# Identity matmuls into an unread PSUM bank, between TensorE's steps in the two closing stages of a two-layer transformer tower

## What is computed

```python
out = attn.reshape(b, n, f) @ W_out + b_out      # 192 x 192
h = h + out
x = _layernorm(h, axis=-1)                       # input of the experts
route = jax.nn.softmax(x @ router_w + router_b)  # 8 experts
```

## Time and profile before

| | |
|---|---|
| median of 3 runs | 1840.75 us (1835.26 to 1847.22) |
| the profiled execution's own time | 1849.49 us |
| its span, first to last instruction | 1847.8 us |
| mean granted clock of TensorE over the span | 0.899 |
| TensorE busy in the span | 1621.7 us (88%) |
| VectorE, ScalarE, GpSimd busy | 1098.9, 613.7, 429.0 us |
| closing stage 0, first to last record | 748.76 to 829.36 us |
| closing stage 1, first to last record | 1315.48 to 1411.91 us |

### The profile page before, as it was taken

How to read it: one execution, slowest core, us unless ns; L and a number is a source line. 1 busy time by engine, 2 the same in 40 slices (tenths; PEclk the granted TensorE clock), 3 DMA queues, 4 the chain that set the end, 5 groups by cost and what they waited for, 6 DMA issues and landing times. The chain is left out here.

```text
span 1847.8 us, 28783 instructions
## 1 busy us (share of the span) xinstructions
PE 1621.7 (88%) x8964; PEld 889.3 (48%) x8965; DVE 1098.9 (59%) x2504; ACT 613.7 (33%) x826; POOL 429.0 (23%) x526
## 2 busy tenths in 40 slices
PE   5759999999899999675999918899699799999998
PEld 3411332233233232473666604667696656666654
DVE  5868998899799891365333335565355823333345
ACT  3411666566566668211111102111012112222111
POOL 6540000000000000101555414000001246666620
PEclk9765999899999999875999958999766799999999
DMA  2480222022222200720111121000420011111124
GB/s 81 148 142 12 35 35 33 4 35 34 35 34 35 35 1 1 212 64 7 39 40 41 36 60 43 2 1 2 120 100 26 1 30 53 52 51 52 46 81 147
DMA packets 64239, 92.82 MB, mean 50 GB/s; under 512 B 9809, under 2 KB 49556, under 8 KB 63124
## 3 DMA queue, kind: packets, MB, share of 16 engines
q1 hardware_dynamic: 50912, 65.08, 15.6%
q0 software_dynamic: 12288, 25.18, 4.6%
q10 hardware_dynamic: 960, 1.57, 0.5%
HBM read 61.82 MB, written 29.98 MB: 50 GB/s over the span
## 5 line engine op out<-in xcount | busy, mean ns | idle before, releaser
L510 DVE TENSOR_REDUCE sa_half_max<-psum 128x1 f32<-128x512 f32 x768 | 494.7, 688 | 79.9 <-PE psum L613 60.0
L567 ACT ACTIVATE sa_probs<-psum 128x1024 f32<-128x1024 f32 x384 | 372.5, 1021 | 168.1 <-PE psum L604 166.6
L613 PE MATMUL psum<-k_stack,q_stack 96*128 96x512 bf16 x768 | 286.4, 411 | 28.8 <-PEq L404 18.8
L604 PE MATMUL psum<-q_stack,k_stack 97*128 97x512 bf16 x768 | 232.1, 386 | 6.1 <-ACT sa_probs L567 5.4
L613 PEld LDWEIGHTS psum<-k_stack,q_stack 96*128 96x128 bf16 x768 | 75.2, 98 | 285.0 <-issue 153.1
L636 PE MATMUL psum<-sa_probs,sa_v_ext 128*32 128x512 f32 x1536 | 207.4, 612 | 0.6 <-ACT sa_probs L567 0.6
L1541 PE MATMUL psum<-w_e_up_a,ex_xt 128*128 x448 | 171.4, 525 | 0.0
L1405 ACT ACTIVATE ex_silu<-psum 128x384 f32<-128x384 f32 (+1 forms) x112 | 59.3, 529 | 289.4 <-PE psum L1541 286.9
L1557 PE MATMUL psum<-w_e_down,ex_g_t 128*128 x752 | 137.2, 334 | 0.5 <-DVE ex_g_t L1437 0.5
L1557 PEld LDWEIGHTS psum<-w_e_down,ex_g_t 128*128 128x128 f32 x752 | 120.7, 190 | 34.5 <-issue 34.5
L1445 DVE COPY ex_to_rows<-slot_rows 128x2 uint32 (+1 forms) x56 | 10.3, 184 | 211.6 <-DMA y_rows<-ex_y,ex_to_rows 117.5
(11 more groups left out here) (267 smaller groups left out, 2257.0 us busy)
## 6 DMA issues: line engine op xcount, KB each, us to landing
q_stack<-qk_parts SPq DMA_DIRECT2D x66, 128.0 KB, 4.5
k_stack<-qk_parts SPq DMA_DIRECT2D x66, 128.0 KB, 7.2
qk_parts<-ep_parts SPq DMA_DIRECT2D x16, 384.0 KB, 3.4
x_tokens<-x SPq DMA_DIRECT2D x16, 384.0 KB, 2.6
ex_rows<-y_rows SPq DMA_DIRECT2D x16, 384.0 KB, 4.7
qk_parts<-ep_parts SPq DMA_DIRECT2D x16, 192.0 KB, 4.3
w_e_down<-e_down SPq DMA_DIRECT2D x1, 3072.0 KB, 32.7
ra_rows<-y_rows SPq DMA_DIRECT2D x8, 384.0 KB, 3.3
```

The source lines that it names most:

```text
L510: nc.vector.tensor_reduce(half_max[:, g, hd, qt, half:half + 1], slot, AX.X, ALU.max).then_inc(ring_free[r], 1)
L567: nc.scalar.activation(probs[:, st % 2, 2 * pair:2 * pair + 2, :], ps[:, 2 * pair:2 * pair + 2, :], ACT.Exp, scale=SCALE0).then_inc(exp_do ...
L604: last = nc.tensor.matmul(ps[:, hd, :], kst[:, g, hd, kt * P:(kt + 1) * P], qst[:, g, hd, half * HALF:(half + 1) * HALF], start=True, stop ...
L613: last = nc.tensor.matmul(ps[:, 4 + r, :], qst[0:SK, g, hd, qt * P:(qt + 1) * P], kst[0:SK, g, hd, half * 512:(half + 1) * 512], start=Tru ...
```

## The change

A bank of PSUM that nobody reads in these stages (7) gets a name, and a helper `stay_warm` issues four 128x128 matmuls of the identity with itself into it. TensorE's step calls it after `project_out`, after `transpose_x2` and after `transpose_rows`, also where a part is left out at the ends. It waits for no semaphore and signals none.

```diff
-        PS_A, PS_B, PS_O, PS_XA, PS_XB, PS_L = 0, 1, 2, 4, 5, 6
+        PS_A, PS_B, PS_O, PS_XA, PS_XB, PS_L, PS_IDLE = 0, 1, 2, 4, 5, 6, 7
+        WARM = 4
...
+            def stay_warm():
+                for _ in range(WARM):
+                    nc.tensor.matmul(ps[:, PS_IDLE, 0:P], s.ident[:], s.ident[:], start=True, stop=True)
+
             def step(this, prev, nxt):
                 project_out(*this)
+                stay_warm()
                 if prev:
                     transpose_x2(*prev)
+                stay_warm()
                 if nxt:
                     transpose_rows(*nxt)
+                stay_warm()
                 if prev:
                     compute_logits(*prev)
```

## The result

The changed kernel takes 1864.40 us (median of 4 runs, 1861.84 to 1866.98) beside 1838.63 us for the kernel before (4 runs, 1835.26 to 1847.22): ratio 1.0129, 95% interval [1.0102, 1.0155]. It is slower by over 1%.

The account below looks back on a forecast made before the run. TensorE was taken to bound both closing stages, layer 1 at half clock and layer 0 with one large hole. Layer 0's +10.7 and layer 1's +10.0 us make +20.7 on the median 1840.75: 1861 us, own range 1854 to 1872, overall 1843 to 1878.

Parts of the forecast that it names:

- the side that had the larger chance: Whole kernel: slower by over 1% was given 0.55, within 1% 0.42, faster by over 1% 0.03.
- two stretches that were to show it: Closing stages: layer 0 about 91 us against 80.6, layer 1 about 106 us against 96.4.
- The price of a record: Each added matmul is two records, 0.12 us each at full clock, 0.215 at half; a group 0.96 or 1.72 us.
- Layer 0: Closing stage of layer 0: 12.0 us paid behind the hole, 1.3 won back; +10.7 us, between +8.0 and +18.9.
- the hole: Layer 0, step 3: TensorE stands 10.73 us while VectorE awaits the x_tokens store; ten groups, 9.6 us, fit free.
- the tail: End of layer 0: last transposes and logits, at half clock before, give back 0 to 2.6 us; 1.3 taken.
- Layer 1, middle steps: Layer 1, steps 1 to 6: two keep the clock, four lose it; 69.0 us against 63.4, +5.6.
- Layer 1, steps 0 and 7: Layer 1's ends: two groups at half clock in step 0, +3.4 us; step 7 +1.0 us.
- The base: The +20.7 us was summed on the profiled execution's 1849.49 us, then put onto the median, 1840.75 us.
- the clock is kept: Rival: layer 1's logits no longer cost the clock, five of six middle steps keep it; 1842 us, chance 0.20.
- Groups that don't count: Rival: groups do not lift the clock, layer 1's first two groups and transposes stay at half; 1886 us, chance 0.10.
- Groups in waits for nothing: Rival: groups fill TensorE's waits free while the clock rises, so faster; within 0.04 for something else.

Follow-up runs that it names:

- e2: The changed kernel with the groups in layer 0 alone, beside the kernel before: 1850.49 us, ratio 1.0058.
- e1: The kernel before, run once more with a profile and without an edit: one execution of 1844.31 us.
- e3: The changed kernel with the groups in layer 1 alone, beside the kernel before: 1855.81 us, ratio 1.0085.
- e5: The kernel before plus, in layer 1 alone, two identity matmuls behind each of the first three logits tiles: 1847.25 us, ratio 1.0040.
- e4: The changed kernel with each added matmul streaming 8 columns instead of 128, beside the kernel before: 1938.42 us, ratio 1.0535.
- e9: The kernel before with layer 1's logits matmuls sorted, those on 128 rows first, then the upper 64; none added: 1834.52 us, ratio 0.9966.
- e8: The kernel before with layer 1's logits computed a step later and their four tiles spread over the step; none added: 1870.35 us, ratio 1.0162.

## Why the prediction was right

1861.0 us was forecast and 1864.4 measured, inside the forecast's own range and on the side that had the larger chance. Of the two stretches that were to show it, that of layer 0 came as named (90.05 us for about 91) and that of layer 1 was 5 us shorter (101.24 for about 106). Step by step:

- *The price of a record.* Taken as 0.12 us at full and 0.215 us at half clock; it is 0.111 and 0.214 (1.71/8). A group is 0.89 instead of 0.96 us. The row of 512-column matmuls, which was the lower end, was nearer than the surplus added to it.
- *Layer 0.* Ten groups were put into the hole: 9.6 us of 10.73. The wait shrank by 7.47 us to 3.26; the stage lost 0.6 us up to the hole's end, and 8.7 us behind it. There, 12.0 us less 1.3 in the tail had been forecast. From the hole's end to the next project_out it was 1.3 us instead of 3.4: the first group took 1.52 us (790.47 to 791.99), and behind it the transposes of the attention rows and the second group were at full clock already. Steps 4 to 6 paid 7.4 us instead of 8.6. From the start of step 7 to the end both kernels take 15.13 us, where 1.3 us were to be won: the last transposes gave back some 0.9 of the 2.6 us and the logits none, and this just paid for what the groups cost beyond the waits. Together +9.3 in the trace and +10.7 us [6.3, 14.9] in e2, for a forecast of +10.7.
- *Layer 1, middle steps.* Two kept at 9.9 us and four lost at 12.3 us were taken, 69.0 us; the trace has two at 9.6, one at 11.2 and three at 12.9, 69.1 us. The mechanism is there in outline: in or behind logits that nothing covers the clock is lost, and it is back before the next logits. Where it comes back differs from step to step, which the forecast had as one case: in the step of 11.2 us within project_out (the first group takes 0.89 us), in the step from 1348.14 within the first group (1.64 us), in the one shown above with the third or fourth transpose, and in the one from 1394.73 only in the second group, so that its eight transposes of the normed rows ran at half (1.70 us). project_out took 4.2 to 5.3 us in these four, for the 4.38 of the earlier trace rows. The lost steps are 12.5 us on average, the kept ones 0.3 us cheaper than taken. That two were kept was a guess; the unchanged stage kept two in e1 and in e2 as well, so the groups need not be the reason.
- *Layer 1, steps 0 and 7.* Here the forecast paid too much in the trace: +3.4 and +1.0 us were taken, +0.8 and -1.6 came. In step 0 project_out did bring the clock back, before the first group, which the earlier trace rows had shown for layer 0 and the forecast had excluded for layer 1. In order of time:

```profile
1334.05 0.71 PE L871 MATMUL psum<-ca_wo_b,ca_rows_tb 65*128 65x192 f32 x2
1334.59 1.95 PE L888 MATMUL psum<-ident 128*128 128x128 f32 x16
1336.38 0.27 PE L845 MATMUL psum<-ident,ca_rows 128*128 128x128 f32 x1
```

  Sixteen records take 1.79 us there, the price at full clock. Step 7 kept its clock too, so its groups lay in the time up to the last normed rows, for which TensorE still waits 0.93 us now. Both are the same in the trace of e3.
- *The base.* The trace has +13.8 us against a forecast sum of +20.7, and the times +25.8. The sum was made against the profiled execution of before, whose stage 1 (93.3 us) is the longest of the three measured of the same code; against 86.3 us the same +4.8 would be +11.8, and e3 gives +15.6 [10.3, 21.0] for the layer, for the +10.0 that were forecast. So the nearness of the hit is in part luck: the sum was 6.9 us too high for its own trace and 5.1 us too low for the medians, and the median of before came out 2.1 us lower with its fourth run. That the profiled execution of before had less of the clock than the others was measured (0.899 against a median of 0.907, see e1); that stage 1 is where they differ is inferred from e1 and e2, not seen, and stays open.

The rivals: *the clock is kept* fell, with 0.80 in the stage and three of six steps at 12.9 us. It had asked for five of six kept. e5 comes near that, with cover right among the logits, and shows that keeping the clock by added matmuls costs as much as it brings. A group directly behind the logits, ahead of project_out, was not tried. *Groups that don't count* fell with the transposes behind them (clock 0.91 in 1388.44:1392.30) and with e4, where groups of 8 columns do what that rival said. *Groups in waits for nothing* was true of the hole and, at the ends of the stages, of single waits.

## What to carry to other kernels

Matmuls that only keep TensorE's clock up are paid at their full streaming price wherever the engine isn't waiting: here 0.89 us a group, and the +0.06 and +0.19 of mean clock (+0.10 in layer 1 if the unchanged stage of e2 is taken) did not return it. Here a stage that stood at 0.61 to 0.70 did not lose enough to its clock to pay for that. It was cheaper to shorten the pieces that lose the clock (sorting the short matmuls by their rows, e9) than to add to them; and whoever rearranges them must look at both ways of the clock, how it is lost and how it returns, since in e8, with the long streams broken up, it never returned. Compare such stages over many runs: the same code's stage 1 differed by 7 us between profiled executions, more than the 4.8 us between the traces of before and after.

## What had not been expected of the hardware

- Eight-column matmuls whose loads take turns between 128 rows and the upper 64 step by 0.157 us a record; sorted, the same ones step by 0.12 us (e9), at full clock both times.
- At half clock a record of 8 columns with a full load costs 0.196 us (1.57/8), one of 128 columns 0.214 us: nearly the same price, but with the former the two stages stood at 0.54 and 0.55 and with the latter at 0.89 and 0.80 (e4 and the change).
- TensorE busy for 97% of a step can stay at half clock for the rest of a stage, when long and short streams take turns (e8, 0.50 throughout 1363.21:1376.20; e4, 0.54 over a whole stage).
